# Copying x into the output in interleaved pairs of pieces with 4 KB runs

## What is computed

```python
h = jnp.maximum(_layernorm(x, axis=-1), 0.0)
x = x + _L0_gnn_ref(h, bases, comps, alpha, stack([src, dst]), edge_type_50)

# in _L0_gnn_ref, row = src and col = dst
deg = segment_sum(ones, row);  deg_inv = where(deg > 0, rsqrt(max(deg, 1)), 0)
norm = deg_inv[row] * deg_inv[col]
hj_b = comps[edge_type][:, :, None] * h[col][:, None, :]
msg = einsum('ebd,bdf->ef', hj_b, bases) * alpha[edge_type] * norm[:, None]
out = segment_sum(msg, row)
```

## Time and profile before

| | us |
|---|---|
| median of 3 runs | 745.38 |
| lowest, highest | 742.51, 745.63 |
| the profiled execution's own time | 752.15 |
| its span in the profile | 750.2 |
| busy: DVE, PE, POOL, ACT | 596.4, 574.7, 540.3, 370.1 |

### The profile page before, as it was taken

One profiled execution on the slowest core, in us unless ns is written; L12 is line 12 of the kernel. 1 busy time (PEld: TensorE's weight loads), 2 busy tenths in 40 slices (PEclk: granted clock), 3 DMA queues, 4 the chain that ended last, 5 costly groups with the idle time before them and its releaser, 6 DMA issues.

```text
span 750.2 us, 13642 instructions
## 1 busy us (share of the span) xinstructions
PE 574.7 (77%) x3922; PEld 406.0 (54%) x3922; DVE 596.4 (80%) x2624; ACT 370.1 (49%) x1494; POOL 540.3 (72%) x404
## 2 busy tenths in 40 slices
PE   4999985665676876987778788886797878888860
PEld 4666654443454645655556565655565656665430
DVE  7999995466775676886987899986998999998730
ACT  0345542244424678664545655645656534446530
POOL 3788886455555587778788888878878767767775
PEclk9999998687788899999998999999999999999995
DMA  8999999989833335444535455444455545544332
GB/s 272 287 326 339 331 361 323 319 296 327 307 101 81 70 54 122 79 92 69 109 52 100 92 86 95 96 81 95 82 95 96 92 78 78 86 57 82 35 36 25
DMA packets 56574, 108.89 MB, mean 145 GB/s; under 512 B 9339, under 2 KB 48264, under 8 KB 55684
## 3 DMA queue, kind: packets, MB, share of 16 engines
q0 software_dynamic: 34496, 25.72, 25.6%
q1 hardware_dynamic: 4416, 50.68, 18.7%
q10 hardware_dynamic: 17588, 31.62, 13.5%
HBM read 94.89 MB, written 64.61 MB: 213 GB/s over the span
## 4 chain that ended last, share of the span: by engine, by line
DVE 14%; DMA 13%; issue 10%; PE 9%; POOL 8%; ACT 7%; ACTq 0%; POOLq 0%
DMA out_dram<-acc,scatter_idx 11%; POOL out_dram L393 6%; DVE masked L481 4%; DVE part_sum L518 4%; PE pst L756 3%; PE pst L737 3%; DVE turned_hot L475 2%; POOL rows L372 2%; DVE same L537 2%; ACT acc L651 2%; DMA rows<-in_x_dram,dst_i 2%; DVE rows L518 2%; ACT scratch L603 2%; PE pst L764 1%; ACT scratch L595 1%
## 5 line engine op out<-in xcount | busy, mean ns | idle before, releaser
L393 POOL DMA_INDIRECT out_dram<-acc,scatter_idx x196 | 313.8, 1601 | 106.3 <-issue 53.7
L372 POOL DMA_INDIRECT rows<-in_x_dram,dst_i x196 | 224.4, 1145 | 96.4 <-issue 36.2
L737 PE MATMUL pst<-table_bits,turned_hot 128*128 128x198 f16 x1568 | 183.1, 267 | 84.0 <-DVE masked L481 61.1
L756 PE MATMUL pst<-bases_sb,h_turned 128*128 128x512 f32 x392 | 214.1, 629 | 0.0
L737 PEld LDWEIGHTS pst<-table_bits,turned_hot 128*128 128x128 f16 x1568 | 147.3, 105 | 113.6 <-issue 59.1
L518 DVE SCALAR_TENSOR_TENSOR part_sum<-pst,coef,part_sum 128x128 f32<-128x128 f32 x392 | 115.7, 343 | 96.2 <-ACT part_sum L641 89.3
L764 PEld LDWEIGHTS pst<-rows,same 128*128 128x128 f32 x392 | 73.0, 199 | 166.2 <-issue 152.1
L641 ACT ACTIVATE part_sum<-pst,coef 128x128 f32<-128x128 f32 x196 | 71.2, 363 | 183.4 <-PE pst L756 132.3
L481 DVE SCALAR_TENSOR_TENSOR masked<-iota_h,lo,pst 128x198 f32<-128x198 f16 x392 | 141.9, 415 | 20.9 <-PE pst L737 16.3
L764 PE MATMUL pst<-rows,same 128*128 128x128 f32 x392 | 82.7, 294 | 58.4 <-ACT acc L651 57.4
L651 ACT ACTIVATE acc<-pst,sum_scale 128x128 f32<-128x128 f32 x196 | 71.5, 365 | 58.5 <-DMA out_dram<-acc,scatter_idx 28.9
(11 more groups left out here) (71 smaller groups left out, 415.8 us busy)
## 6 DMA issues: line engine op xcount, KB each, us to landing
out_dram<-in_x_dram SPq DMA_DIRECT2D x46, 1000.0 KB
src_row<-src_rows ACTq DMA_DIRECT2D x25, 512.0 KB
edge_row<-edge_rows ACTq DMA_DIRECT2D x45, 256.0 KB
out_dram<-in_x_dram ACTq DMA_DIRECT2D x4, 1000.0 KB
rows<-in_x_dram,dst_i POOLq DMA_INDIRECT x196
out_dram<-acc,scatter_idx POOLq DMA_INDIRECT x196
rows<-edge_rows ACTq DMA_DIRECT2D x10, 175.0 KB
edge_row<-edge_rows SPq DMA_DIRECT2D x4, 256.0 KB
```

Source lines behind the costliest of these rows:

```text
L372: pool.indirect_dma_start(row(t), None, x, bass.IndirectOffsetOnAxis(ap=dst_i[:, t:t + 1], axis=0)) \
L393: pool.indirect_dma_start(out, bass.IndirectOffsetOnAxis(ap=scatter_idx[:, t:t + 1], axis=0), acc[:, t % ACC_RING, :], None, compute_op=AL ...
L737: last = pe.matmul(pst[:, LOOK + t % 2, k * LO:(k + 1) * LO], turned_hot[:, g % 2, c, k * W + j * P:k * W + (j + 1) * P], table[:, c * LO: ...
L756: pe.matmul(pst[:, PRODUCT + t % 4, :], h_turned[:, g % 2, j, :], bases_sb[:].rearrange("d b f -> d (b f)"), start=True, stop=True).then_i ...
```

## The change

Pieces come in pairs. A pair covers 4,096 rows (2 MB). It is seen as 256 blocks of 16 rows; the even piece takes the first eight rows (4 KB) of each block, the odd piece the other eight. So a piece is 2,048 rows (1.049 MB) in 256 runs of 4 KB with a step of 8 KB, and both sides of the DMA have this form. There are 24 pairs and one last piece of 1,696 rows (0.868 MB), seen as before as one contiguous run in 32 rows: 49 pieces for 50. Who issues them, and the two in flight, stay. As the number of pieces is odd, the final waits count 25 pieces on one semaphore and 24 on the other.

```diff
-    COPIES = 50
-    COPY_ROWS = N // COPIES
+    RUN_ROWS, RUNS = 8, 256
     COPY_RING = 2
+    PAIR_ROWS = 2 * RUNS * RUN_ROWS
+    COPIES = 2 * (N // PAIR_ROWS) + 1
+    LAST_COPY = (COPIES // 2) * PAIR_ROWS
...
-            a = i * COPY_ROWS
-            flat_out, flat_x = (y[a:a + COPY_ROWS, :].rearrange("r d -> (r d)") for y in (out, x))
-            engine.dma_start(flat_out.rearrange("(q e) -> q e", q=32), flat_x.rearrange("(q e) -> q e", q=32)) \
-                .then_inc(copied[i % COPY_RING], 16)
+            if i < COPIES - 1:
+                a = i // 2 * PAIR_ROWS
+                to, of = (y[a:a + PAIR_ROWS, :].rearrange("(q s r) d -> s q (r d)", s=2, r=RUN_ROWS)[i % 2]
+                          for y in (out, x))
+            else:
+                to, of = (y[LAST_COPY:N, :].rearrange("r d -> (r d)").rearrange("(q e) -> q e", q=32)
+                          for y in (out, x))
+            engine.dma_start(to, of).then_inc(copied[i % COPY_RING], 16)
+
+        def copies_done(engine):
+            for b in range(COPY_RING):
+                engine.wait_ge(copied[b], 16 * len(range(b, COPIES, COPY_RING)))
...
-            for b in range(COPY_RING):
-                sp.wait_ge(copied[b], 16 * (COPIES // COPY_RING))
+            copies_done(sp)
...
-            for b in range(COPY_RING):
-                pool.wait_ge(copied[b], 16 * (COPIES // COPY_RING))
+            copies_done(pool)
```

More of the change, by code:

```diff
@@ L111, in sums_at @@
         return list(range(a + (b - a) * j // GROUP, a + (b - a) * (j + 1) // GROUP))
-    COPIES = 50
-    COPY_ROWS = N // COPIES
+    RUN_ROWS, RUNS = 8, 256
     COPY_RING = 2
+    PAIR_ROWS = 2 * RUNS * RUN_ROWS
+    COPIES = 2 * (N // PAIR_ROWS) + 1
+    LAST_COPY = (COPIES // 2) * PAIR_ROWS
     FIRST_COPIES = 4
-    assert COPIES * COPY_ROWS == N and COPIES % COPY_RING == 0
+    assert LAST_COPY < N and (N - LAST_COPY) * D % 32 == 0
     rows16_dram = nc.dram_tensor("edge_rows", (3, TILES * P), F16, kind="Internal").ap()
```

## The result

The changed kernel takes 773.11 us (median of four runs, 772.21 to 776.06) against 745.07 for the kernel before, measured beside it: a ratio of 1.039, 95% interval 1.0353 to 1.0427. It is 28 us slower, where 5 us faster was forecast, and outside the range of 735 to 757. The profiled execution took 776.06 us, of which 774.0 are its span.

What follows compares the result with a forecast made beforehand. POOL's arrival at scatter 11, set by the later of computation and copy, was taken to bound the kernel. Computation 5.5 us earlier, less 0.5, with the copy's +6 hidden by slack, gave 745.38 - 5 = 740.4 us; range 735 to 757.

Steps and rivals of the forecast that it cites:

- What bounds the kernel: POOL's arrival at scatter 11 fixes the time: the later of computation (257.8 us) and copy's end plus some 32 us.
- The slack of 13.5 us: At scatter 11: the copy allowed 244.3 us, the computation 257.8, so a copy later by up to 13.5 us costs nothing.
- The price of 16 times the packets: On the DMA engines: 690 packets more on each make the copy 6 us longer, hidden by slack.
- My upper bound of +48 us: Longest lengthening of the copy, priced from POOL's gathers under the copy at 69 ns for each of 690 packets.
- The late copy: Rival, chance 0.20: each 4 KB run costs its engine 30 ns extra, the copy ends at 233 us, time 755.
- The bad step: Rival, chance 0.04: the 8 KB step is bad for the memory; the copy at half its rate gives about 907 us.
- Waits behind the copy: Before 210 us, gathers, edge rows and instructions wait less behind shorter copy packets: computation 5.5 us earlier, from 0 to 7.4.
- The rule that I weighed there: An engine drains a packet of 9 to 17 descriptors before changing rings; turns could stay long and the gain be zero.
- the 5.5 us for the computation: Three quarters of 7.4 us of DVE idleness before 210 us, expected to go with shorter copy packets.

Runs made afterwards that it cites:

- the copy alone: Two kernels holding only copies from SP, one shape to a stretch; twelve pieces took 55 to 57 us with a step of 8 KB, 41.73 in 64,000 B packets.
- 12 KB steps: Changed kernel with three pieces interleaved in place of two, 4 KB runs kept: 749.91 us, ratio 0.9977 against the kernel before.
- dealt: Changed kernel with each piece one contiguous 1 MB whose 4 KB runs go round to the 16 engines: 748.84 us, ratio 1.0057 against the kernel before.
- 8 KB runs: Changed kernel with runs of 16 rows, step 16 KB: 740.17 us, ratio 0.9966 against the kernel before; again 742.62 us, ratio 0.9981.

## Why the prediction was wrong, step by step

**What bounds the kernel.** Right. POOL's 31.7 us to scatter 11 came out to 0.1 us, and the length from there to the last gather to 3 us: 333.4 and 331.2 in the changed kernel, 330.5 and 330.4 before. Where the copy is what POOL waits for, the span is the first scatter's date plus 523 to 527 us: 247.24 and 774.0, 250.31 and 773.2, 223.68 and 746.9, 213.32 and 737.6.

**The slack of 13.5 us.** A real number, but of one execution. It accounts for that pair of profiles: 34.6 us of delay less 13.5 is the 21.1 of scatter 11. In the second profile of the kernel before the first scatter is at 211.81 and scatter 11 at 255.18, which leaves 11.7 us; in the third they are at 213.92 and 250.41: 4.8 us. It was worked out from one profile that lay 6.8 us above the median, and I said so, but scaled the sum without asking which stretch held those 6.8 us.

**The price of 16 times the packets.** The step that failed: "I take +6 us, by ACT's rows: they are nearest in kind and size." For the packets alone it was near: 10 ns each in the copy alone and 8 in the kernel with 12 KB steps, for the 9 to 17 of the earlier trace rows. But those rows hold runs that lie side by side, and the changed copy's lie 8 KB apart. SP's queue was busy 21.9% of 774.0 us = 169.5. On the page of the kernel before its row is

```profile
q1 hardware_dynamic: 4416, 50.68, 18.7%
```

which is 140.3 us of 750.2. These 29 us, where I had +6, are most of the 34.6 by which the first scatter came later; between the third profile of the kernel before and the second of the changed one, on one chip, they are 35 of 36.4. My upper bound of +48 us held; my range did not use it.

**The rivals.** The late copy, at 0.20, had the right place and nearly the size of the price (30 ns; 39 measured), but by the wrong mechanism, and it reached only 755; the range ended at 757, short of what my bound of +48 us allowed. The bad step, at 0.04, was the cause; I priced it as half the rate, 907 us, and set it aside: "For it I have no row." The loss alone is 56.0 for 41.9 us, a quarter of the rate. The Trainium skill's page "DMA: Bandwidth & Descriptors", section "Latency and other measured facts", has copies at row pitches from 512 KiB up, and I read it as clearing small ones: the runs show a loss at a step of 8 KB, of which that section says nothing.

**Waits behind the copy.** "With 4,096 B in a packet, I estimate a turn of the copy at 0.18 us ... and most of the 6.4 us gone": wrong for gathers. Over the groups that waited before 120 us, the median from a gather's start to its statistics is 6.5, 7.2 and 7.5 us in three profiles of the kernel before, 7.3 and 7.4 changed, 6.1 dealt, 6.8 with 12 KB steps and 6.6 and 6.7 with 8 KB runs. The 9.5 us behind my 8.0 (33.68 to 41.68, counted from the gather's end) were the worst of that profile, taken for the rule. For example in the kernel after:

```profile
80.80 1.47 POOL L383 DMA_INDIRECT rows<-in_x_dram,dst_i  x1 [0.30 <-PE pst L733]
87.95 0.31 ACT L605 ACTIVATE scratch<-rows 128x128 f32<-128x128 f32 x1 [5.07 <-DMA rows<-in_x_dram,dst_i]
```

What a gather waits for with two pieces in flight is then not the length of one packet. The rule that I weighed there, of the Trainium skill's page "DMA: Bandwidth & Descriptors", section "Queues, rings and completion order", with 9 to 17 descriptors of one ring at a time, agrees with this; the runs don't show it by itself. Nor is it the queued bytes alone: with four pieces in flight gathers took up to 43 us in 64,000 B packets and 7 to 8 in packets of 4 and 8 KB. What makes the difference there stays open. Of the 5.5 us for the computation 1.4 to 4.9 were seen in the first sum, in single executions and with the clock as a rival; that sooner edge rows are the reason isn't shown.

**The late first type row** was in no term. DVE's instruction for it starts 3 to 4 us later in the changed kernel (27.37 and 27.82 us, for 24.03 to 24.41), hidden like all of the computation behind the copy.

**As a sum**: a computation 1 to 5 us earlier and +6 for the packets would have given about the kernel before. That is what 4 KB packets without the step do: 0.2% faster with 12 KB steps, which isn't clear of noise, and 0.6% slower dealt. The step of 8 KB makes the rest. Without it the forecast of 5 us faster would still have missed, by 3 to 9 us.

## What to carry to other kernels

Price the addresses of a DMA, not only its size: two copies of equal bytes, equal packets and equal count differed by a third, and a row with the same size of packet says nothing on a step that it doesn't have. A loop of pieces over each candidate shape, alone in a kernel, gives that price in one run, before anything is built on it. And a slack read in one profile is that execution's: hold it against the stretch in which the execution differs from the others before spending it.

## What the runs showed of the hardware that I had not expected

- DRAM-to-DRAM copies in runs of 4 KB with a step of 8 KB: twelve pieces in 55 to 57 us against 41.9 without gaps or 42.9 with a step of 12 KB; with the step on the read side alone 9.1 us are lost, on the write side alone 3.6. The shape of 2 KB runs with a step of 4 KB is mildly slow (34.0 us for eight pieces, against 28.9), with twice the packets.
- In a copy alone, a packet of 4 KB holds an engine 196 ns, and the same bytes in a 64,000 B packet 186.
- A view of 32 contiguous rows went as 16 packets of 64,000 B (256 packets with their semaphores for eight pieces). Gaps between runs, or an order that isn't the memory's, kept the runs apart: 256 packets of 4 KB to a piece, also where the pieces are dealt.
- Doubling the pieces in flight from two to four, with 64,000 B packets, stretched a gather from 6 to 8 us up to 43 and made the kernel 6.9% slower, though the engines moved as many bytes from 80 to 100 us (345 GB/s for 351). With 4 KB and 8 KB packets gathers stayed at 7 to 8 us.
- The kernel before had a median of 752.6 us in one comparison and of 743.6 to 745.1 in the four others, so only ratios taken side by side say something here.
